# A two-layer model on one core: GpSimd's product in place in a ring of six, TensorE's adds three units later, norm 6 on ScalarE, step sizes in earlier units

## What is computed

```python
h = x @ fc1_w.T + fc1_b
xc, z = jnp.split(h @ in_proj_w.T, 2, axis=-1)
u = jax.nn.silu(causal convolution of xc over 4 steps + conv_b)
dt_low, Bm, Cm = jnp.split(u @ x_proj_w.T, [8, 24], axis=-1)
dt = jax.nn.softplus(dt_low @ dt_proj_w.T + dt_proj_b)
A = -jnp.exp(A_log)

def step(hstate, t):
    dt_t, B_t, C_t, u_t = t
    dA = jnp.exp(dt_t[..., None] * A)
    hstate = dA * hstate + (dt_t * u_t)[..., None] * B_t[:, None, :]
    return hstate, jnp.einsum('bdn,bn->bd', hstate, C_t)

y = scan of step over 1024 positions + u * D
out = ((y * jax.nn.silu(z)) @ out_proj_w.T) @ fc2_w.T + fc2_b
x = x + out
x = x + feed_forward(layernorm(x))
```

## Time and profile before

| | |
|---|---|
| median of three runs | 1117.55 us |
| lowest, highest | 1115.35, 1117.87 us |
| the profiled execution | 1121.12 us |
| its span | 1119.8 us |
| PE busy | 1066.3 us (95%), 6860 matmuls |
| DVE busy | 839.1 us (75%) |
| ACT busy | 630.4 us (56%) |
| POOL busy | 763.4 us (68%) |
| granted TensorE clock, mean | 0.991 |

### The profile page before, as it was taken

One profiled execution on the slowest core, in us unless ns is written; L12 is line 12 of the kernel. 1 busy time (PEld: TensorE's weight loads), 2 busy tenths in 40 slices (PEclk: granted clock), 3 DMA queues, 4 the chain that ended last, 5 costly groups with the idle time before them and its releaser, 6 DMA issues.

```text
span 1119.8 us, 18526 instructions
## 1 busy us (share of the span) xinstructions
PE 1066.3 (95%) x6860; PEld 662.1 (59%) x6860; DVE 839.1 (75%) x1234; ACT 630.4 (56%) x898; POOL 763.4 (68%) x394
## 2 busy tenths in 40 slices
...
DMA packets 55369, 68.91 MB, mean 62 GB/s; under 512 B 23248, under 2 KB 41424, under 8 KB 55280
## 3 DMA queue, kind: packets, MB, share of 16 engines
...
q0 software_dynamic: 1024, 2.10, 0.6%
...
## 4 chain that ended last, share of the span: by engine, by line
PE 79%; issue 7%; DVE 6%; POOL 4%; ACT 3%; DMA 1%; another core or an unknown queue 1%; POOLq 0%; DVEq 0%; ACTq 0%
PE psum L661 20%; PE psum L622 16%; PE psum L647 6%; PE psum L635 5%; PE psum L1046 3%; PE psum L687 3%; PE psum L952 3%; PE psum L1029 3%; POOL hc L2252 3%; PE psum L746 3%; PE psum L702 2%; PE psum L810 2%; PE psum L821 2%; PE psum L726 2%; PE psum L680 2%
## 5 line engine op out<-in xcount | busy, mean ns | idle before, releaser
L2164 POOL TENSOR_TENSOR psums<-psums,prob 128x1024 f32<-128x1024 f32 x180 | 430.5, 2392 | 26.1 <-POOL psums L2164 0.5
L1627 DVE TENSOR_REDUCE mx<-psum 128x2 f32<-128x1024 f32 x256 | 299.8, 1218 | 102.0 <-PE psum L647 101.6
L1158 ACT ACTIVATE prob<-psum 128x1024 f32<-128x1024 f32 x256 | 261.3, 1026 | 62.6 <-PE psum L635 38.1
L661 PE MATMUL psum<-prob,V 128*64 128x512 f32 x1024 | 238.7, 597 | 0.0
L2252 POOL TENSOR_TENSOR hc<-hs,cc 128x1024 f32<-128x1024 f32 x64 | 151.6, 2368 | 21.1 <-DVE hs L1930 18.6
L1930 DVE TENSOR_TENSOR_SCAN hs<-dA,psum 128x1024 f32<-128x1024 f32 x64 | 146.3, 2287 | 2.2
L661 PEld LDWEIGHTS psum<-prob,V 128*64 128x64 f32 x1024 | 67.7, 137 | 106.7 <-issue 105.0
L2164 POOL TENSOR_TENSOR psums<-prob 128x1024 f32<-128x1024 f32 x30 | 72.1, 2403 | 85.0 <-ACT prob L1158 84.2
L1177 ACT COPY oraw<-psum 128x512 f32<-128x512 f32 x32 | 18.8, 587 | 191.3 <-PE psum L661 191.3
L952 PE MATMUL psum<-hc,ident 128*128 128x512 f32 x256 | 122.5, 601 | 2.8 <-DVE slot_rows_h L1938 1.4
L647 PE MATMUL psum<-k_hi,q_hi 64*128 64x512 f32 x512 | 107.0, 409 | 1.7 <-DVE mx L1627 1.3
...
## 6 DMA issues: line engine op xcount, KB each, us to landing
...
```

The lines of the kernel that those rows point to most:

```text
L661: ins = pe.matmul(A.O[HALF[s], :], A.V[pair % 2][:, j, s * DH:(s + 1) * DH], A.prob[unit(pair, c, j) % NPB][:, s * CH:(s + 1) * CH], start ...
L1158: act.activation(A.prob[n % NPB][:, :], slots.bank("score", pair, c, j).rearrange("p s n -> p (s n)"), ACT.Exp, scale=float(DH) ** -0.5).t ...
L1627: dve.tensor_reduce(K.A.mx[:, :, t, c], slots.bank("max", pair, t, c), AXX, ALU.max).then_inc(*slots.inc("max", pair, t, c))
L2164: pool.tensor_tensor(total[:, :], (K.A.prob[(n - 1) % NPB] if j == 1 else total)[:, :], K.A.prob[n % NPB][:, :], ALU.add).then_inc(*K.psum ...
```

## The change

It has three parts. The buffers `hc` are gone: POOL writes the product over the state in `hs`, which has six buffers (`NHS`), PE adds from there, and scan u now waits for add u-6 instead of product u-3 (POOL's wait for an add goes). PE's adds come three units after their spread's step instead of two (`ADD_LAG`), so the last three adds stand together behind unit 63; the skips move with them, and so do `leave` and `gated` for both halves of batch 0 and DVE's output of half (1, 0). Norm 6 takes the way of norm 5: `half_at(g)` gives norm 5 for g of 0 and 1, and norm 6 for 2 and 3. The step sizes of the last half, (1, 1), are computed in units 30 to 38 instead of 40 to 45.

```diff
@@ -61,6 +61,8 @@
 EARLY_UPS = 14
 
 PRE_EW = 11
+
+NHS, ADD_LAG = 6, 3
 
 LAST_ROWS, LAST_BANK = (B - 1, SEQ // CH - 1), B * (SEQ // CH) * M1 - 1
 
@@ -381,15 +383,15 @@
            10: [("fc1", 1, 0), ("fc1_out", 1, 0), ("readd", 1), ("readd_out", 1), ("means", 1), ("centre", 1)],
            11: [("mix", 0, 0, 0), ("squares", 1), ("halfroot", 1)], 12: [("mix", 0, 1, 0), ("mix", 0, 2, 0), ("halfrows", 1), ("du", 0, 1)],
            13: [("mix", 0, 3, 0)], 14: [("lnturn", 5, 1), ("lncopy", 5, 1)], 15: [("fc1", 1, 1), ("fc1_out", 1, 1)],
-           16: [("mix", 1, 0, 0), ("mix", 1, 1, 0)], 17: [("leave", 0, 0), ("gated", 0, 0), ("mix", 1, 2, 0), ("mix", 1, 3, 0)],
-           18: [("silu", 1, 0, 0), ("silu", 1, 1, 0)], 19: [("mix", 0, 0, 1), ("mix", 0, 1, 1)], 20: [("mix", 0, 2, 1)],
+           16: [("mix", 1, 0, 0), ("mix", 1, 1, 0)], 17: [("mix", 1, 2, 0), ("mix", 1, 3, 0)],
+           18: [("leave", 0, 0), ("gated", 0, 0), ("silu", 1, 0, 0), ("silu", 1, 1, 0)], 19: [("mix", 0, 0, 1), ("mix", 0, 1, 1)], 20: [("mix", 0, 2, 1)],
            21: [("mix", 0, 3, 1), ("mix", 1, 0, 1), ("fc2bias", 0)], 22: [("mix", 1, 1, 1)], 23: [("mix", 1, 2, 1), ("mix", 1, 3, 1)],
            24: [("silu", 1, 0, 1), ("silu", 1, 1, 1), ("xpj", 1, 0)], XDR_UNIT: [("xpj", 1, 1), ("xpj_out", 1), ("xdr", 1)],
-           26: [("dtp", 1, 0), ("dtp_out", 1, 0)], 27: [("softexp", 1, 0)], 28: [("softlog", 1, 0), ("dt", 1, 0)], 29: [("du", 1, 0)],
-           33: [("leave", 0, 1), ("gated", 0, 1)], 35: [("outp", 0, 0)], 36: [("outp_out", 0, 0), ("outp", 0, 1)], 37: [("outp_out", 0, 1), ("fc2", 0, 0)],
-           38: [("fc2", 0, 1), ("fc2_out", 0, 0)], 39: [("fc2_out", 0, 1)], 40: [("lnvar", 6), ("lnroot", 6), ("dtp", 1, 1)],
-           41: [("dtp_out", 1, 1), ("lnrows", 6)], 43: turned(6)[:2] + [("softexp", 1, 1), ("softlog", 1, 1), ("fc2bias", 1)],
-           44: turned(6)[2:] + [("dt", 1, 1), ("inp", 1, 2)], 45: [("inp_out", 1, 2), ("du", 1, 1)], 46: [("inp", 1, 3)],
+           26: [("dtp", 1, 0), ("dtp_out", 1, 0)], 27: [("softexp", 1, 0)], 28: [("softlog", 1, 0), ("dt", 1, 0)], 29: [("du", 1, 0)], 30: [("dtp", 1, 1)], 31: [("dtp_out", 1, 1)], 32: [("softexp", 1, 1), ("softlog", 1, 1)],
+           34: [("leave", 0, 1), ("gated", 0, 1)], 35: [("outp", 0, 0)], 36: [("outp_out", 0, 0), ("outp", 0, 1), ("dt", 1, 1)], 37: [("outp_out", 0, 1), ("fc2", 0, 0)],
+           38: [("fc2", 0, 1), ("fc2_out", 0, 0), ("du", 1, 1)], 39: [("fc2_out", 0, 1), ("means", 2), ("centre", 2)], 40: [("squares", 2), ("halfroot", 2), ("means", 3), ("centre", 3)],
+           41: [("halfrows", 2)], 42: [("squares", 3), ("halfroot", 3)], 43: [("halfrows", 3)] + turned(6)[:2] + [("fc2bias", 1)],
+           44: turned(6)[2:] + [("inp", 1, 2)], 45: [("inp_out", 1, 2)], 46: [("inp", 1, 3)],
            47: [("inp_out", 1, 3), ("w1hi", 0), ("w1lo", 0), ("xhi", 0, 0), ("xlo", 0, 0)], 55: [("xhi", 0, 1), ("xlo", 0, 1)]}
     for e in range(E1):
         one[48 + e - 1] = one.get(48 + e - 1, []) + [("w1hi", e), ("w1lo", e)] * (e > 0)
@@ -949,7 +951,7 @@
             pe.matmul(X.Y[:, c * CH:(c + 1) * CH], X.skip[:, k, :], X.u[b][:, k, c * CH:(c + 1) * CH], start=False, stop=False)
     pe.wait_ge(X.product_done, u + 1)
     for c in range(NC):
-        ins = pe.matmul(X.Y[:, c * CH:(c + 1) * CH], K.ident[:, :], X.hc[u % 3][:, c * CH:(c + 1) * CH],
+        ins = pe.matmul(X.Y[:, c * CH:(c + 1) * CH], K.ident[:, :], X.hs[u % NHS][:, c * CH:(c + 1) * CH],
                         start=(u > 0 and n == 0), stop=(n == NS - 1))
     ins.then_inc(X.added, 1)
 
@@ -969,10 +971,11 @@
         pe_spread_B(K, pe, 0)
     if u + 1 < RECS:
         pe_spread_B(K, pe, u + 1)
-    if u > 1:
-        pe_add_state(K, pe, u - 2)
+    if u >= ADD_LAG:
+        pe_add_state(K, pe, u - ADD_LAG)
     if u == RECS:
-        pe_add_state(K, pe, u - 1)
+        for v in range(RECS - ADD_LAG + 1, RECS):
+            pe_add_state(K, pe, v)
 
 
 def pe_outp(K, pe, b, c):
...
@@ -1195,27 +1198,40 @@
     act.copy(K.x[:, at, :], K.work.bank("readd", c).rearrange("p (t d) -> p t d", d=D)).then_inc(*K.work.inc("readd", c))
 
 
+def half_at(g):
+
+    n, first = (LN_SSM + 1, NT) if g < 2 else (LN_E1, 0)
+    return n, first, range(4 * (g % 2), 4 * (g % 2) + 4)
+
+
+def ln_count(n):
+    return n - (n > LN_SSM + 1) - (n > LN_E1)
+
+
 def act_half_rows(K, act, g):
 
+    n, first, ts = half_at(g)
     act.wait_ge(K.X.rooted, g + 1)
-    for t in range(4 * g, 4 * g + 4):
-        ins = act.activation(K.xrows[:, NT + t, :], K.x[:, NT + t, :], ACT.Identity, scale=K.rstd[:, t:t + 1], bias=K.shift[:, t:t + 1])
-    ins.then_inc(*K.act_rows.inc(LN_SSM + 1, g))
+    for t in ts:
+        ins = act.activation(K.xrows[:, first + t, :], K.x[:, first + t, :], ACT.Identity, scale=K.rstd[:, t:t + 1], bias=K.shift[:, t:t + 1])
+    ins.then_inc(*K.act_rows.inc(n, g % 2))
 
 
 def act_means(K, act, g):
 
-    act.wait_ge(*K.work.empty("readd", g))
-    for t in range(4 * g, 4 * g + 4):
-        ins = act.activation(K.xrows[:, NT + t, :], K.x[:, NT + t, :], ACT.Identity, scale=1.0 / D, accum_out=K.mv[:, t, 0:1])
+    n, first, ts = half_at(g)
+    act.wait_ge(*(K.work.empty("readd", g) if g < 2 else K.work.empty("fc2", 0, g - 2)))
+    for t in ts:
+        ins = act.activation(K.xrows[:, first + t, :], K.x[:, first + t, :], ACT.Identity, scale=1.0 / D, accum_out=K.mv[:, t, 0:1])
     ins.then_inc(K.X.means_done, 1)
 
 
 def act_squares(K, act, g):
 
+    n, first, ts = half_at(g)
     act.wait_ge(K.X.centred, g + 1)
-    for t in range(4 * g, 4 * g + 4):
-        ins = act.activation(K.xrows[:, NT + t, :], K.x[:, NT + t, :], ACT.Square, bias=K.shift[:, t:t + 1], accum_out=K.mv[:, t, 1:2])
+    for t in ts:
+        ins = act.activation(K.xrows[:, first + t, :], K.x[:, first + t, :], ACT.Square, bias=K.shift[:, t:t + 1], accum_out=K.mv[:, t, 1:2])
     ins.then_inc(K.X.squares_done, 1)
 
 
...
@@ -1921,13 +1937,13 @@
     if u == 0:
         dve.wait_ge(X.dt_done, 1)
     dve.tensor_tensor(X.gain[u % 2], X.gain[u % 2], (X.du if u else X.dt)[b][:, k, :], ALU.mult).then_inc(X.gain_done, 1)
-    if n == 2 and u > (KI + 1) * NS:
+    if n == ADD_LAG and u > (KI + 1) * NS:
         dve_output(K, dve, *divmod(u // NS - 1, KI))
     dve.wait_ge(X.gain_done, u + 1)
     dve.wait_ge(X.decay_done, u + 1)
-    if u >= 3:
-        dve.wait_ge(X.product_done, u - 2)
-    dve.tensor_tensor_scan(X.hs[u % 3][:, :], X.dA[u % 3][:, :], X.gain[u % 2], 0.0, ALU.mult, ALU.add).then_inc(X.state_done, 1)
+    if u >= NHS:
+        dve.wait_ge(X.added, u - NHS + 1)
+    dve.tensor_tensor_scan(X.hs[u % NHS][:, :], X.dA[u % 3][:, :], X.gain[u % 2], 0.0, ALU.mult, ALU.add).then_inc(X.state_done, 1)
 
 
 def dve_output(K, dve, b, k):
@@ -2014,7 +2030,7 @@
     elif n == 0:
         engine.wait_ge(K.X.state_done, RECS)
     elif n == 3:
-        engine.wait_ge(K.X.product_done, RECS)
+        engine.wait_ge(K.X.added, RECS - (RECS - 1) % NHS)
 
 
 def dve_split1(K, dve, n):
...
@@ -2121,7 +2137,7 @@
 
 def pool_half_root(K, pool, g):
 
-    at, own = slice(4 * g, 4 * g + 4), K.pool_own
+    at, own = slice(4 * (g % 2), 4 * (g % 2) + 4), K.pool_own
     pool.wait_ge(K.X.squares_done, g + 1)
     pool.tensor_scalar(K.std[:, at], K.mv[:, at, 1], 1.0 / D, LN_EPS, ALU.mult, ALU.add).then_inc(*own.inc())
     pool.wait_ge(*own.now())
...
@@ -2243,13 +2259,11 @@
     if u == 0:
         pool.wait_ge(*K.work.empty("down", LAST_KQ))
     pool.wait_ge(X.C_spread[u % NCC], 16 * (u // NCC + 1))
-    if u >= 3:
-        pool.wait_ge(X.added, u - 2)
     if u:
         pool.wait_ge(X.product_done, u)
     if u == XDR_UNIT + 1:
         pool.wait_ge(X.xdr_done, B)
-    pool.tensor_tensor(X.hc[u % 3][:, :], X.hs[u % 3][:, :], X.cc[u % NCC][:, :], ALU.mult).then_inc(X.product_done, 1)
+    pool.tensor_tensor(X.hs[u % NHS][:, :], X.hs[u % NHS][:, :], X.cc[u % NCC][:, :], ALU.mult).then_inc(X.product_done, 1)
 
 
 def pool_w1(K, pool, e):
@@ -2597,8 +2611,8 @@
             X.soft = [[X.tmp[:, :], X.xc[:, 0, 0:SEQ]] for _ in range(B)]
             X.C_rows = internal("C_rows", (B, NS, SEQ))
             X.xdr = [sba(f"xdr{b}", [P, SEQ], F32R) for b in range(B)]
-            X.dA, X.hs, X.hc, X.cc = ([sba(f"{n}{i}", [P, SEQ]) for i in range(k)] for n, k in
-                                      (("dA", 3), ("hs", 3), ("hc", 3), ("cc", NCC)))
+            X.dA, X.hs, X.cc = ([sba(f"{n}{i}", [P, SEQ]) for i in range(k)] for n, k in
+                                      (("dA", 3), ("hs", NHS), ("cc", NCC)))
 
 
         with ExitStack() as scope:
```

More of the change, by code:

```diff
@@ L1183, in act_rows @@
     b = n % 2
-    act.wait_ge(K.ln_root, n - (n > LN_SSM + 1))
+    act.wait_ge(K.ln_root, ln_count(n))
     for t in range(NT):
```

6 lines of the change are left out of this document (3 added, 3 removed).

## The result

| | before | with the change |
|---|---|---|
| median of 17 executions | 1117.56 us (1115.35 to 1119.76) | 1121.48 us (1117.89 to 1125.29) |
| ratio, 95% interval | | 1.0033 [1.0024, 1.0043] |
| profiled execution: time, span | 1121.12, 1119.8 us | 1123.18, 1121.9 us |
| scan 0 to scan 63 | 226.17 us | 229.81 us |
| from scan 63's start to the end | 103.14 us | 104.97 us |

The change makes the kernel 3.9 us slower, three times the forecast +1.2, and inside the range, near its upper end. Ratio and interval go over all executions of both kernels, so they can say up to 0.9 us more or less than the medians. The last two lines of the table split the profiled executions: 1.83 us behind the last scan, where the forecast had 1.75, and 3.64 us over the recurrence, where it had -0.56. (The profiled recurrence began 3.4 us earlier, at 787.12, so the spans are only 2.1 us apart.)

What follows compares the result with a forecast made beforehand. VectorE was taken to bound the recurrence (790 to 1019 us), TensorE what follows. Recurrence -0.56 plus end +1.75 gave +1.2 us, carried to the median of 1117.55: 1118.8 us; 8-in-10 range 1114.5 to 1122.0.

Steps and rivals of the forecast that it cites:

- Clock, the first rival: TensorE's clock halves behind norm 6's second transpose, losing 2.5 us: +3.7 in all, 1121.3 us; chance 0.05.
- the side above 1120.9 us: Outcome slower by over 0.3%, made up of the clock and late-GpSimd rivals; chance 0.18.
- a late GpSimd: At unit 34 or 42, one more product (2.37 us) ahead in GpSimd's queue delays TensorE: +3.6, 1121.1 us; chance 0.13.
- Part 1, ring and product in place: Recurrence: scans wait for add u-6, product keeps 2.37 us; worth 0, bounds 0 to -3.26 us.
- Part 2, statistics: Norm 6's 16 small instructions leave VectorE's path for ScalarE, where they cost 0: -2.21 us.
- Part 3, lag and steps: Recurrence: adds three units later and the steps moved behind them; +0.88, +1.47 and -0.70 us.
- +0.88: Around unit 35: TensorE stands 2.4 us for du before outp, +0.43, and the next outp cycle adds +0.45 us.
- +1.47: Around units 43 to 48, norm 6: 0.1 for gain 45, +0.45 at spread 46, +0.92 at gain 48.
- -0.70: Two old waits of VectorE for spreads at 958.81 and 962.71, 0.25 and 0.45 us from scan to scan, go.
- 0 within 0.2: Unit 15 loses a 0.66 us wait for product 13; unit 19 waits for ScalarE's copy and a silu instead.
- Part 4, the end: Behind the last scan: one add more left over, +1.72, +0.40 for spread 63, -0.37 idle: +1.75 us.
- the lag does what its shape promises: Rival: all six VectorE waits for a spread vanish, -3.7 in all, 1113.8 us; chance 0.10.

Runs made afterwards that it cites:

- e11: Kernel before the change, plus only 10 filler matmuls (results overwritten) on TensorE ahead of the wait for norm 5's rows; ratio 0.9997 to the kernel before.
- e6: The change itself, unaltered, measured and profiled a second time; 1121.50 against 1118.27 us for the kernel before, ratio 1.0027.
- e1: The change with adds two units later again and leave and gated back in units 17 and 33; 1122.37 against 1122.29 us for the kernel before, ratio 1.0000.
- e5: e1 plus 10 filler matmuls each ahead of the waits for norm 5's and norm 6's rows; 1115.35 against 1118.27 us for the kernel before, ratio 0.9974.
- e4: The change plus filler matmuls on TensorE, 12 ahead of norm 5's first-half rows and 8 before outp; ratio 1.0026 to the kernel before.
- e10: The change with outp one unit later, two units of lag at the end, 10 fillers each ahead of norm 5's and 6's rows; ratio 0.9992 to the kernel before.
- e12: e5 with 9 fillers ahead of norm 5's rows and 12 ahead of norm 6's; 1116.85 against 1117.77 us for the kernel before, ratio 0.9984.
- e2: Kernel before the change with only the ring of six and the product written in place; ratio 1.0001 to the kernel before.
- e3: e2 plus adds three units later (leave and gated in units 18 and 34), old statistics and step-size places; ratio 1.0041 to the kernel before.
- e9: The change with adds three units later up to unit 51 and two from unit 52 on; ratio 1.0021 to the kernel before.

## Why the prediction was right in direction and short in size

**Where clocks fell.** All unfilled waits of these kinds in the eleven profiles of kernels that have them, in how many the clock fell to 0.50, and the cost on the path when it did:

| wait of TensorE before | length | fell | cost |
|---|---|---|---|
| norm 5's transpose, adds two late | 2.55 us | 3 of 4 | 1.7 to 2.2 us (against e11, against before) |
| the same, adds three late | 3.00 | 4 of 5 | 1.67 (the change against e6) |
| outp (0, 0) in unit 35, adds three late | 2.22 | 3 of 4 | 1.66 |
| norm 6's second transpose, statistics on ScalarE | 2.93 to 3.02 | 3 of 6 | 1.68 (e1 2.15, e5 0.47) |
| spread 43, statistics on VectorE | 3.22 | 3 of 5 | 0 (scan 41 has 2.20 either way) |

Nine filled waits (norm 5 in e4, e5, e10, e11, e12; norm 6 in e5, e10, e12; outp in e4) fell never. The change adds the third and fourth line: 0.75 x 1.66 + 0.5 x 1.68 = 2.1 us on the mean. Without falls it costs 0.28 + 1.7 = 2.0 (e6). The sum, 4.1, is near what was measured, 3.9 and 3.2. The 2.0 is shown piece by piece in traces; that falls make up the rest of the median is argued, not shown. The frequencies are from few executions, and by them e4 should have saved 2.6 us, less 0.3, where it saved 0.1 to 0.8, and e11 some 1.3 where its ratio says 0.3: they are likely too high.

**Clock, the first rival: the step that failed.** "The two new standstills ... are shorter than 3.22, so I price the clock at 0." One row at 1.00 behind one wait was read as a rule. At the same wait of 3.22 us the clock fell in three of the four other profiles. The rival had the mechanism, a place and a price of 2.5 us (1.7 measured) and was given 0.05; it should have had two places and the larger part of the chance. The Trainium skill, "TensorE: Matmul & The Clock Gate", section "Why this matters for your kernels", warns of idle gaps of TensorE between matmul bursts, but only above a length that waits of 2.22 and 2.55 us don't reach. Here the clock fell at six of eight of these, so the measurement decides. That the range held is in part luck: the time lies on the side above 1120.9 us that had 0.18, most of it for a late GpSimd, which didn't come.

**Part 1, ring and product in place: 0.** Right (e2, 2365 against 2368 ns).

**Part 2, statistics: -2.21.** Right in place: scan 41's excess of 2.21 is gone, and the decay for scan 43 ended 4.8 us ahead of it, the cover that was forecast. Its row in the change (the scan started at 945.43):
```profile
939.45 1.13 ACT L1403 ACTIVATE dA<-slotT,alog 128x1024 f32<-128x1024 f32 x1
```
But 0.9 us of it come back at scans 45 to 48, which have 1.6 us of excess in e5, with the adds two units late, as in the change, and 0.7 in e3, with them three late and the old statistics. The prediction has nearly this sum, 1.47 - 0.70, but puts it down to part 3; it belongs to norm 6's new way, whose net gain is so 1.3 us.

**Part 3, lag and steps: +0.88, +1.47, -0.70.** Right in places and sizes, where no clock fell: TensorE stood 2.22 us for du (2.4 forecast), scans 37 and 38 have 0.53 and 0.43 (0.43, 0.45); it stood 2.93 between norm 6's transposes (3.0), and scans 45, 46 and 48 have 0.25, 0.45 and 0.91 (0.1, 0.45, 0.92). Its "0 within 0.2" for units 15 and 19 holds too. What it missed are early scans that it took as unchanged or didn't name: scans 26 to 28 have 1.11 to 1.15 us instead of 0.62, in e3 (statistics as before) as well, while e1 with two units of lag hasn't got it. Scans 11 and 12 have 0.45 more in e6 than in the first profile of before; e11 has 0.35 more without any lag, but with a filler, so whether that is the lag's stays open. With these 0.96 us, less 0.3 at other early scans, the recurrence without falls is 0.28 us longer (e6) and not 0.56 shorter.

**Part 4, the end: +1.75.** Right: 104.83 to 104.97 us behind the last scan in each kernel with three units to the end, 103.05 to 103.20 in each with two, and e9 moves it by itself.

**The other rivals.** No product came late and no scan waited for an add. The lag removed no early wait for a spread; "the lag does what its shape promises" is refuted by e3 and e10.
